# A two-layer graph network on one core: the last row panel's gated unit and its last two tiles by halves, its stores on the load queue, and another order of the row panels

## The chip, the cores and the metric

The kernel runs on one core of a Trainium2 chip. The metric is the device time of one execution, in microseconds (us). Before the change it was 1813.91 us, the median of three runs (1813.1 to 1814.12).

## What is computed

The inputs are `x` (8192 x 128), a weighted adjacency matrix `adj` (8192 x 8192, fp32, 256 MB) and small weights. Cut to what matters:

```python
# layer 0: degree-normalised aggregation, residual, layer norm
dinv = rsqrt(sum(adj, axis=1) + 1e-6)
x1 = layernorm(x + (dinv[:, None] * (adj + I) * dinv[None, :]) @ (x @ W0))
# layer 1: aggregation, message, gated recurrent unit, residual, layer norm
agg = adj @ x1
msg = relu(agg @ W_msg.T + b_msg)
r = sigmoid(msg @ Wir.T + x1 @ Whr.T + b_r)
z = sigmoid(msg @ Wiz.T + x1 @ Whz.T + b_z)
n = tanh(msg @ Win.T + b_in + r * (x1 @ Whn.T + b_hn))
out = layernorm(x1 + (1 - z) * n + z * x1)
```

## The kernel before

**Tiles.** The rows are cut into 16 row panels of W = 512 rows; a tile (i, k) is the 512 x 512 block of row panel i and neighbour panel k, 1 MB, loaded transposed so that the 512 output rows are the free dimension. Features are on the 128 partitions. The matrix is read twice. The first pass (to about 680 us) sums the degrees and already multiplies what it can for layer 0. The second pass is a list `T2` of 256 tiles, one index n per tile: tiles 0 to 103 (N2 = 104) serve layer 0 and layer 1, tiles 104 to 255 (NN = 256) layer 1 alone, row panel after row panel in the order `rows3` (line 183).

**One tile of the second pass.** SP loads it in two halves of 512 KB (L380). ACT writes its rounded part `hi` in fp32r (L678), DVE the rest `lo` = tile - hi (L826), and PE does three products for each of the four 128-row chunks c, hi with x1's high part (L495), lo with the high part (L496), hi with x1's low part (L497): twelve matmuls 512 columns wide, each with its own 128 x 128 weights. `hi` has three buffers: ACT writes tile n when PE is done with tile n - 3. The accumulator `acc1` alternates between two PSUM banks (6 and 1) from row panel to row panel.

**The gated unit of a row panel.** When the last tile of panel i is multiplied (index `gru_at[i]`, lines 192 to 195; at least 9 tiles after that of the panel before), its steps are dealt out over the following tile indices, on each engine behind the tile work of that index: x1 transposed back by eight 128-column products with an identity (`x1t_step`, PE +1, L552 and L554), its copies `x1t` and `x1th` (ACT +5, L714, L715) and `x1tl` (DVE +5, L913), the aggregate `tall` (DVE +3, L902), the message (`msg_step`, PE +4, L562, fp32), the three products with the state (`h_step`, PE +5) and with the message (`gates_step`, PE +6; nine matmuls each, L566 to L568), the two sigmoids (ACT +9, L728, L729), the candidate's two DVE steps (+9, L925, L928), tanh (ACT +11, L733), the new state in three dependent DVE steps (+11, L936, L938, L940), its transpose by four 128 x 128 products (`rows_step`, PE +11, L594), statistics (DVE +14, L835, L839), the reciprocal deviation on POOL (L1041, L1043), the scaling to `y` (DVE +16, L845), and the store, 256 KB, issued by POOL's software queue (L1055). Each of these steps has 512 columns, or four times 128.

After tile 255 nothing is left but the steps of the last panel (panel 7, `gru_at` = 256) and the rest of panel 8's (`gru_at` = 247): the loops run on to index NN + TAIL with TAIL = 17. At the end POOL waits for the stores (L1057), every engine drains, and a barrier (L229) ends the kernel.

**Order.** Each engine works off its own list in order, and the only coupling are semaphores. SP's list holds the loads alone. POOL's holds the deviations and stores. The lines that set the row order and the places of the unit:

```python
    rows3 = [15, 0, 14, 1, 13, 2, 12, 3, 11, 4, 10, 5, 9, 6, 8, 7]
    gru_at, g = {}, -100
    for i in rows3:
        g = max(end3[i], g + 9)
        gru_at[i] = g
    TAIL = gru_at[rows3[-1]] + 17 - NN
```

By these lines the sixteen units stand at 119, 128, 139, 148, 157, 166, 175, 184, 193, 202, 211, 220, 229, 238, 247 and 256.

Of the kernel before, what the change touches and what calls it, by code (L numbers as in the profile page):

```python
# [5 lines left out]
def gnn_resnorm_kernel(nc, adj_blocks, x_t, x, w0, wmsg_t, b_msg, wih_t, whh_t, b_ih, b_hh, out):  # L6
    f32, f32r = mybir.dt.float32, mybir.dt.float32r
    ALU, ACT = mybir.AluOpType, mybir.ActivationFunctionType

    D = 128  # L10
# [182 lines left out]
    for i in rows3:  # L193
        g = max(end3[i], g + 9)
        gru_at[i] = g
    TAIL = gru_at[rows3[-1]] + 17 - NN

    norm_rows = whole[::-1] + rows2
    norm_no = {i: q for q, i in enumerate(norm_rows)}
# [3 lines left out]
        return next((i for i in rows2 if end2[i] + d == n), None)  # L203

    def gru_row(n, d):
        return next((i for i in rows3 if gru_at[i] + d == n), None)

    RING2, RING3 = [0, 1, 2, 3], [0, 1, 2, 3, 15, 16]
    slot_of2, before2, loads2 = [], [], []
# [19 lines left out]
    with ctx:  # L229
# [3 lines left out]
        def sem(name):  # L233
            return ctx.enter_context(nc.semaphore(name))
# [127 lines left out]
        nmul_done, npre_ready, n_ready = sem("nmul_done"), sem("npre_ready"), sem("n_ready")  # L362
        diff_done, new_ready, rows_done = sem("diff_done"), sem("new_ready"), sem("rows_done")
        out_ready = sem("out_ready")

        def group_left(eng, g):

# [5 lines left out]
        @block.sync  # L373
        def _(sp):
            def load(s, i, k):

                P, Q, rows = i // 2, k // 2, (i % 2) * W
                for h in range(2):
                    src = adj_blocks[P * 8 + (P - Q) % 8, 2 * (k % 2) + h, :, :, rows:rows + W]
                    sp.dma_start(raw(s)[:, 2 * h:2 * h + 2, :], src).then_inc(slot_in[s], 16)  # L380

            def load_xt(P):
                if P:
                    sp.wait_ge(supp_done, P)
# [24 lines left out]


        @block.tensor
        def _(pe):
# [175 lines left out]
            def rows_step(i):  # L588
                g = gru_no[i]
                pe.wait_ge(new_ready, g + 1)  # L590
                if g:
                    pe.wait_ge(out_ready, g)
                for c in range(KC):
                    mm = pe.transpose(p_rows[:, c * D:(c + 1) * D], newt[:, c * 128:(c + 1) * 128], ident[:, :])  # L594
                mm.then_inc(rows_done, 1)


            turn(whole[1])
            for R, j in burst[last][2:]:
# [2 lines left out]
            turn(whole[0])  # L602
            layer0(1)
            layer1(0)
            for n in range(1, NN + TAIL):
                if 2 <= n < N2:
                    layer0(n)
                i = normed_row(n, 1)
                if i is not None:
                    turn(i)  # L610
                if n < NN:
                    layer1(n)
                i = gru_row(n, 1)
                if i is not None:
                    x1t_step(i)
                i = gru_row(n, 4)
                if i is not None:
                    msg_step(i)
                i = gru_row(n, 5)
                if i is not None:  # L620
                    h_step(i)
                i = gru_row(n, 6)
                if i is not None:
                    gates_step(i)
                i = gru_row(n, 11)
                if i is not None:
                    rows_step(i)


        @block.scalar  # L630
        def _(act):
# [99 lines left out]
            def n_step(i):  # L731
                act.wait_ge(npre_ready, gru_no[i] + 1)
                act.activation(gn[:, :], gn[:, :], ACT.Tanh, bias=bih_s[:, 2:3]).then_inc(n_ready, 1)  # L733

            for P in range(NP):
# [9 lines left out]
            x1_hi(whole[1])  # L745
            hi_f0(2)
            x1_hi(whole[0])
            for n in range(3, NN + TAIL):
                if n < NN:
                    hi_tile(n)  # L750
                    hi_f0(n)
# [12 lines left out]
                if i is not None:  # L764
                    msg_step(i)
                i = gru_row(n, 9)
                if i is not None:
                    rz_step(i)
                i = gru_row(n, 11)
                if i is not None:  # L770
                    n_step(i)


        @block.vector
        def _(dve):
# [178 lines left out]
            def half_out(h):  # L954
# [6 lines left out]
                rows = part[:, (2 * groups[g][0] + h) * W:(2 * groups[g][0] + h + 1) * W]  # L961
                dve.tensor_copy(rows, group_bank(g, h)[:, :]).then_inc(last_out, 1)

            split_lo(0)
            split_lo(1)
            own_step(whole[1])
# [10 lines left out]
            for n in range(2, NN + TAIL):  # L977
                if n < NN:
                    split_lo(n)
                i = normed_row(n, 2)  # L980
                if i is not None:
                    tall_step(i)
                    if i // 2 >= SELF_PANELS:
                        own_step(i)
                i = normed_row(n, 3)
                if i is not None:
                    row_step(i)
                i = normed_row(n, 4)
                if i is not None:
                    x1_step(i)  # L990
                i = normed_row(n, 5)
                if i is not None:
                    x1_lo(i)
                i = gru_row(n, 3)
                if i is not None:
                    agg_step(i)
                if n == N2 // 4:
                    split_weights()
                i = gru_row(n, 5)
                if i is not None:  # L1000
# [92 lines left out]
```

## Time and profile before

| | |
|---|---|
| runs | 1813.91 us (median of 3; 1813.1 to 1814.12) |
| profiled execution, its own time | 1815.5 us |
| its span in the trace | 1813.6 us |
| mean granted clock of TensorE | 0.972 |
| PE / DVE / ACT / POOL busy | 92% / 80% / 40% / 8% of the span |
| bytes moved by DMA | 551.11 MB, mean 304 GB/s |

The engines are PE (TensorE matmul; PEld its weight loads, which overlap), DVE (VectorE), ACT (ScalarE), POOL (GpSimd) and SP (SyncE, which issues loads). L826 is line 826 of the kernel. The span runs from the first to the last instruction of the trace; the execution's own time is 1.9 us longer, and a difference between two kernels is read in either. A chain of waits is followed back from the last instruction. A timeline lists instructions with start and duration; the duration of a matmul runs to its last result, so back-to-back matmuls overlap, and the distance of two starts is what one costs.

### The profile page before, as it was taken

The numbers are of one execution on the slowest core, as the hardware profiler recorded it, in microseconds if no ns is written. First come the engines' busy times: TensorE is split into PE (matmuls) and PEld (weight loads), VectorE is DVE, ScalarE is ACT, GpSimd is POOL, SyncE is SP. The second block draws the span as 40 slices with busy tenths as digits, with TensorE's granted clock in tenths as the row PEclk, the third lists the DMA queues.
The fourth block names the chain that finished last, engine by engine and source line by source line (L and its number), as shares of the span: only waits on it lengthen the run. The fifth ranks groups of instructions, "written<-read, shape, count | busy, mean of one in ns | idle before, by whom it ended". The sixth has DMA issues, their size and how long they took to land.

```text
span 1813.6 us, 16909 instructions
## 1 busy us (share of the span) xinstructions
PE 1665.1 (92%) x6400; PEld 1167.1 (64%) x6400; DVE 1448.2 (80%) x1372; ACT 725.6 (40%) x708; POOL 141.5 (8%) x110
## 2 busy tenths in 40 slices
PE   0088799997999999999999999999999999999996
PEld 0043254443444456888888888888788888888884
DVE  7888899999999967776666665665789898988886
ACT  0000011111111123544444444444677676767663
POOL 0000000000000011100000000000002112121212
PEclk8589999999999999999999999999999999999998
DMA  9999999999999982666666666665999999999991
GB/s 389 421 380 422 422 421 422 421 421 422 421 421 421 420 311 85 207 200 204 193 196 199 201 190 195 201 192 188 346 344 322 302 320 308 322 312 317 312 313 52
DMA packets 180928, 551.11 MB, mean 304 GB/s; under 512 B 13424, under 2 KB 13936, under 8 KB 148080
## 3 DMA queue, kind: packets, MB, share of 16 engines
q1 hardware_dynamic: 177280, 541.11, 80.8%
q0 software_dynamic: 2560, 8.39, 1.4%
q8 instruction: 51, 0.84, 0.2%
q10 hardware_dynamic: 1008, 0.53, 0.1%
q14 instruction: 29, 0.24, 0.0%
HBM read 545.79 MB, written 4.19 MB: 303 GB/s over the span
## 4 chain that ended last, share of the span: by engine, by line
PE 82%; DMA 13%; DVE 3%; ACT 1%; issue 0%; POOL 0%; SPq 0%; DVEq 0%; ACTq 0%; POOLq 0%
PE bank L444 21%; PE bank L495 18%; PE bank L497 18%; PE bank L496 18%; DMA kept<-adj_blocks 6%; DMA ring<-adj_blocks 4%; DMA pool<-adj_blocks 3%; PE bank L568 1%; PE bank L566 1%; PE bank L567 1%; DVE colsum L804 1%; PE bank L427 1%; PE bank L418 1%; PE bank L562 1%; PE bank L466 1%; DVE lo L826 0%
## 5 line engine op out<-in xcount | busy, mean ns | idle before, releaser
L826 DVE TENSOR_TENSOR lo<-ring,hi 128x2048 fp32r<-128x2048 f32 x206 | 470.3, 2289 | 249.1 <-ACT f L689 205.0
L678 ACT ACTIVATE hi<-ring 128x2048 fp32r<-128x2048 f32 x206 | 395.3, 1919 | 366.8 <-DMA ring<-adj_blocks 238.4
L495 PE MATMUL bank<-hi,x1s 128*128 128x512 f32 x1024 | 409.4, 400 | 3.8 <-DVE lo L826 2.7
L497 PE MATMUL bank<-hi,x1s 128*128 128x512 f32 x1024 | 399.9, 391 | 0.0
L496 PE MATMUL bank<-lo,x1s 128*128 128x512 f32 x824 | 321.6, 390 | 0.0
L444 PE MATMUL bank<-kept,feat 128*128 128x512 f32 x656 | 292.6, 598 | 20.4 <-DMA kept<-adj_blocks 20.4
L444 PEld LDWEIGHTS bank<-kept,feat 128*128 128x128 f32 x656 | 123.4, 191 | 180.6 <-issue 155.0
L804 DVE TENSOR_TENSOR colsum<-colsum,kept 128x2048 f32<-128x2048 f32 x93 | 213.2, 2292 | 20.0 <-DMA kept<-adj_blocks 18.4
L495 PEld LDWEIGHTS bank<-hi,x1s 128*128 128x128 f32 x1024 | 192.7, 188 | 47.1 <-issue 3.6
L497 PEld LDWEIGHTS bank<-hi,x1s 128*128 128x128 f32 x1024 | 192.6, 188 | 41.1
L656 ACT ACTIVATE part<-bank 128x512 f32<-128x512 f32 x72 | 39.1, 595 | 444.5 <-PE bank L444 444.5
L496 PEld LDWEIGHTS bank<-lo,x1s 128*128 128x128 f32 x824 | 155.2, 188 | 33.1 <-issue 1.7
L495 PE MATMUL bank<-hi,f 128*128 128x512 f32 x416 | 162.4, 390 | 0.0
L497 PE MATMUL bank<-hi,f 128*128 128x512 f32 x416 | 161.9, 389 | 0.0
L496 PE MATMUL bank<-lo,f 128*128 128x512 f32 x416 | 161.8, 389 | 0.0
L444 PE MATMUL bank<-ring,feat 128*128 128x512 f32 x272 | 123.8, 601 | 5.8 <-DMA ring<-adj_blocks 5.8
L826 DVE TENSOR_TENSOR more_lo<-more,hi 128x2048 fp32r<-128x2048 f32 x50 | 114.2, 2285 | 14.1 <-ACT hi L678 14.1
L444 PE MATMUL bank<-pool,feat 128*128 128x512 f32 x256 | 115.3, 595 | 6.8 <-DMA pool<-adj_blocks 6.8
L678 ACT ACTIVATE hi<-more 128x2048 fp32r<-128x2048 f32 x50 | 96.0, 1919 | 50.9 <-PE bank L497 48.4
L1041 POOL TENSOR_TENSOR var<-mv,eps_ln 128x4 f32<-128x4 f32 x32 | 36.0, 1126 | 978.9 <-DVE mv L839 978.9
L444 PEld LDWEIGHTS bank<-ring,feat 128*128 128x128 f32 x272 | 51.6, 192 | 71.5 <-issue 61.7
L804 DVE TENSOR_TENSOR colsum<-colsum,ring 128x2048 f32<-128x2048 f32 x38 | 87.1, 2292 | 9.3 <-DMA ring<-adj_blocks 8.7
(111 smaller groups left out, 1689.2 us busy)
## 6 DMA issues: line engine op xcount, KB each, us to landing
ring<-adj_blocks SPq DMA_DIRECT2D x412, 512.0 KB, 5.3
kept<-adj_blocks SPq DMA_DIRECT2D x147, 1024.0 KB, 14.9
ring<-adj_blocks SPq DMA_DIRECT2D x56, 1024.0 KB, 14.9
pool<-adj_blocks SPq DMA_DIRECT2D x53, 1024.0 KB, 14.6
more<-adj_blocks SPq DMA_DIRECT2D x100, 512.0 KB, 5.8
xt<-x_t SPq DMA_DIRECT2D x8, 512.0 KB, 14.1
xin<-x POOLq DMA_DIRECT2D x16, 256.0 KB, 3.4
out<-y POOLq DMA_DIRECT2D x16, 256.0 KB, 3.7
```

The lines of the kernel that those rows point to most:

```text
L418: mm = pe.matmul(p_supp[c // KC][:, (c % KC) * D:(c % KC + 1) * D], xt[:, c * 128:(c + 1) * 128], w0_s[:, :], start=True, stop=True)
L427: mm = pe.matmul(p_deg[:, b:b + 1], csum[:, b * 128:(b + 1) * 128], ones[:, :], start=True, stop=True)
L444: mm = pe.matmul(group_bank(g, h)[:, :], feat0[:, j * 2 + u, :], unit(slot_of1[n])[:, u, h * W:(h + 1) * W], start=begins and g < NP and u ...
L466: mm = pe.matmul(group_bank(g, h)[:, :], feat0[:, j * 2 + u, :], unit(slot_of1[n])[:, u, h * W:(h + 1) * W], start=False, stop=j == 4 * P ...
L495: pe.matmul(acc[:, :], fh, ah, start=start and c == 0, stop=False, skip_group_check=True)
L496: pe.matmul(acc[:, :], fh, al, start=False, stop=False, skip_group_check=True)
L497: mm = pe.matmul(acc[:, :], fl, ah, start=False, stop=stop and c == KC - 1, skip_group_check=True)
L656: ins = act.activation(part[:, i * W:(i + 1) * W], group_bank(g, h)[:, :], ACT.Copy)
L678: ins = act.activation(hi[:, n % NHI], raw(slot_of2[n]), ACT.Copy)
L804: dve.tensor_tensor(cs, cs, slot(slot_of1[n]), ALU.add).then_inc(sum_done, 1)
L826: ins = dve.tensor_tensor(flat(low(n)), flat(raw(slot_of2[n])), flat(hi[:, n % NHI]).bitcast(f32), ALU.subtract)
L1041: pool.tensor_tensor(var[:, at % 2], mv[:, at % 2, :, 1:2], eps_ln[:, :, :], ALU.add).then_inc(veps_ready, 1)
```

## The change

- The row order `rows3` becomes 10, 2, 12, 0, 11, 1, 14, 7, 3, 4, 15, 6, 8, 5, 9, 13. The units now stand at 115, 124, 133, ... 241, nine apart without exception, and the last panel is 13, with 14 tiles (242 to 255).
- The last panel's unit is written out apart. Its `x1t_step` is at PE's index 252. Its last two tiles are multiplied for columns 0 to 255 first, then for columns 256 to 511, the second time into the other accumulator bank; `last_sum` adds both halves' sum so far, `last_sum2` what the second bank holds.
- All its steps but the x1 copies are done for each half of 256 columns, in other banks (`p_rz2`, `p_n2`, `p_msg2`), interleaved in an order given by hand. The new state takes two steps after tanh instead of three, `(gz - 2) * x1t` before it.
- Its two stores of 128 KB are issued by SP, which has no loads left by then; SP waits for them. POOL waits for the other panels' stores.
- TAIL becomes 2.

```diff
-    rows3 = [15, 0, 14, 1, 13, 2, 12, 3, 11, 4, 10, 5, 9, 6, 8, 7]
+    rows3 = [10, 2, 12, 0, 11, 1, 14, 7, 3, 4, 15, 6, 8, 5, 9, 13]
-    TAIL = gru_at[rows3[-1]] + 17 - NN
+    last_row, G, HW = rows3[-1], NT - 1, W // 2
+    TAIL = gru_at[rows3[-2]] + 17 - NN
+        p_rz2, p_n2, p_msg2 = (bank[0], bank[7]), (bank[2], bank[3]), (bank[4], bank[5])
...
@@ sync
+            for h in range(2):
+                c = last_row * KC + 2 * h
+                sp.wait_ge(out_ready, G + 1 + h)
+                sp.dma_start(out_rows[:, c:c + 2, :], y[:, G % 2, 2 * h:2 * h + 2, :]).then_inc(last_stored, 16)
+            sp.wait_ge(last_stored, 32)
@@ tensor
+            def last_tile(n, h):
+                acc, k = acc1[(len(rows2) + G + h) % 2], T2[n][1]
+                pe.wait_ge(lo_ready, n + 1)
+                if h == 1:
+                    pe.wait_ge(agg_ready, G)
+                for c in range(KC):
+                    ah, al = hi[:, n % NHI, c, half(h)], low(n)[:, c, half(h)]
+                    fh, fl = x1s[:, k * KC + c, 0, :], x1s[:, k * KC + c, 1, :]
+                    pe.matmul(acc[:, half(h)], fh, ah, start=h == 1 and n == NN - 2 and c == 0, stop=False,
+                              skip_group_check=True)
+                    pe.matmul(acc[:, half(h)], fh, al, start=False, stop=False, skip_group_check=True)
+                    mm = pe.matmul(acc[:, half(h)], fl, ah, start=False, stop=n == NN - 1 and c == KC - 1,
+                                   skip_group_check=True)
+                if n == NN - 1:
+                    mm.then_inc(halves_done, 1)
...
-            for n in range(1, NN + TAIL):
+            for n in range(1, NN - 2):
...
+                if n == NN - 4:
+                    x1t_step(last_row)
+            last_tile(NN - 2, 0)
+            last_tile(NN - 1, 0)
+            last_h(0)
+            last_msg(0)
+            last_h(1)
+            last_tile(NN - 2, 1)
+            last_gates(0)
+            last_tile(NN - 1, 1)
+            last_msg(1)
+            last_rows(0)
+            last_gates(1)
+            last_rows(1)
@@ scalar
+            x1t_step(last_row)
+            last_relu(0)
+            last_rz(0)
+            last_n(0)
+            last_relu(1)
+            last_rz(1)
+            last_n(1)
@@ vector
+            def last_npre(h):
+                dve.wait_ge(rz_ready, G + 1 + 2 * h)
+                dve.wait_ge(diff_done, 2 * G)
+                dve.scalar_tensor_tensor(gn[:, half(h)], p_n2[h][:, half(1)], bhh_s[:, 2:3], gr[:, half(h)], ALU.add, ALU.mult)\
+                   .then_inc(nmul_done, 1)
+                dve.wait_ge(nmul_done, G + 1 + h)
+                dve.tensor_tensor(gn[:, half(h)], gn[:, half(h)], p_n2[h][:, half(0)], ALU.add).then_inc(npre_ready, 1)
+                dve.wait_ge(rz_ready, G + 2 + 2 * h)
+                dve.wait_ge(rows_done, G)
+                dve.scalar_tensor_tensor(newt[:, half(h)], gz[:, half(h)], -2.0, x1t[:, half(h)], ALU.add, ALU.mult)\
+                   .then_inc(last_u, 1)
...
+                if n == NN - 1:
+                    x1t_lo(last_row)
                 i = gru_row(n, 14)
                 if i is not None:
                     out_stats(i)
+                if n == NN:
+                    last_sum()
                 i = gru_row(n, 16)
                 if i is not None:
                     out_step(i)
+            last_lo(0)
+            last_npre(0)
+            last_sum2()
+            last_newt(0)
+            last_lo(1)
+            last_norm(0)
+            last_npre(1)
+            last_newt(1)
+            last_norm(1)
@@ gpsimd
-            for g, i in enumerate(rows3):
+            for g, i in enumerate(rows3[:-1]):
...
-            for s in range(2):
-                pool.wait_ge(stored[s], NT // 2 * 16)
+            for h in range(2):
...
+            pool.wait_ge(stored[0], NT // 2 * 16)
+            pool.wait_ge(stored[1], (NT // 2 - 1) * 16)
```

`last_h`, `last_msg`, `last_gates`, `last_rows`, `last_relu`, `last_rz`, `last_n`, `last_lo`, `last_newt` and `last_norm` are the steps of the unit named above for one half: nine, one, nine and two matmuls on PE, two, two and one activations, one DVE step for the low part of the message, two for the new state, and two statistics, two aggregates and two scalings.

## Rows read from the trace of the kernel before

**Rows 1.** The page: span, and PE's granted clock in 40 slices.
```profile
span 1813.6 us, 16909 instructions
...
PEclk8589999999999999999999999999999999999998
```

**Rows 2.** Busy time by stretch, 1380 to 1790 us and behind.
```profile
core 0: us, PE busy (x) PEld busy (x) DVE busy (x) ACT busy (x) POOL busy (x), PEclk, DMA share, GB/s
1380.00:1790.00 410.00, 409.94 (x1855) 334.80 (x1854) 365.16 (x382) 277.18 (x209) 74.63 (x39) 1.00 0.90 303
1790.00:1800.68 10.68, 6.17 (x26) 4.00 (x25) 5.71 (x18) 4.34 (x7) 2.01 (x3) 1.00 0.08 25
1800.68:1813.60 12.92, 1.11 (x4) 0.71 (x4) 4.67 (x15) 0.00 (x0) 2.02 (x3) 0.50 0.07 20
```

**Rows 3.** Waits, 1330 to 1789 us: total us, times, longest us.
```profile
ACT hi L678 <- PE bank L497: 137.5, 130, 2.9
DVE lo L826 <- ACT hi L678: 30.8, 29, 2.5
...
PEld bank L495 <- DVE lo L826: 0.3, 1, 0.3
```

**Rows 4.** Chain of waits behind 1790 us: start, us, what.
```profile
1791.45 1.10 PE bank L562 x2
...
1797.07 0.69 ACT gr L728
...
1802.83 1.13 PE bank L594 x4
...
1808.16 0.74 issue
1808.90 0.80 POOL out L1055
```

**Rows 5.** Timeline of PE at the last tile's end: start, us.
```profile
1788.95 0.39 PE L497 MATMUL bank<-hi,x1s 128*128 128x512 f32 x1
1789.18 0.22 PE L552 MATMUL bank<-identr,x1s 128*128 128x128 f32 x1
1789.24 0.27 PE L554 MATMUL bank<-identr,x1s 128*128 128x128 f32 x1
...
1790.02 0.63 PE L594 MATMUL bank<-ident,newt 128*128 128x128 f32 x4
```

**Rows 6.** Instructions of the closing barrier, L229: ns, start us.
```profile
L229 SPq DRAIN  x1: 369/369/369, 1768.7 to 1768.7; - x1
...
L229 POOLq DRAIN  x1: 1462/1462/1462, 1811.9 to 1811.9; - x1
```

**Rows 7.** Instruction groups by shape, whole run: busy us, mean ns.
```profile
L826 DVE TENSOR_TENSOR lo<-ring,hi 128x2048 fp32r<-128x2048 f32 x206 | 470.3, 2289 | 249.1 <-ACT f L689 205.0 <-ACT hi L678 44.1
L678 ACT ACTIVATE hi<-ring 128x2048 fp32r<-128x2048 f32 x206 | 395.3, 1919 | 366.8 <-DMA ring<-adj_blocks 238.4 <-PE bank L497 128.4
...
L723 ACT ACTIVATE msgh<-bank,bmsg_s 128x512 fp32r<-128x512 f32 x16 | 10.9, 680 | 0.0
...
L902 DVE TENSOR_TENSOR tall<-part,bank 128x512 f32<-128x512 f32 x14 | 9.5, 681 | 0.0
```

**Rows 8.** Timeline of DVE, last statistics and scaling.
```profile
1803.98 0.89 DVE L835 BATCH_NORM_STATS2 stats<-bank 128x6 f32<-128x128 f32 x4 [1.21 <-PE bank L594]
...
1806.78 1.37 DVE L845 TENSOR_SCALAR y<-bank,mv,rstd 128x128 f32<-128x128 f32 x4 [1.49 <-POOL rstd L1043]
```

**Rows 9.** Issue to landing, us: POOL's last store, SP's 512 KB loads (L380).
```profile
DMA to landing us min/median/max: 2.8/2.8/2.8
...
L380 SPq DMA_DIRECT2D ring<-adj_blocks x412: 539/604/1587, 646.7 to 1768.0; - x138
...
DMA to landing us min/median/max: 4.0/5.4/15.6
```

**Rows 10.** DMA, GB/s in 40 slices of 0.05 us from 0.75 us.
```profile
GB/s 0 0 0 0 0 0 0 0 0 0 0 0 0 0 0 0 0 0 0 0 655 492 164 0 0 0 0 0 492 655 164 0 0 0 0 0 0 0 0 0
```

More of the change, by code:

```diff
@@ L195, in gnn_resnorm_kernel @@
         gru_at[i] = g
-    TAIL = gru_at[rows3[-1]] + 17 - NN
+    last_row, G, HW = rows3[-1], NT - 1, W // 2
+    TAIL = gru_at[rows3[-2]] + 17 - NN
+    assert end3[last_row] == NN - 1 and last_row in rows2 and gru_at[rows3[-2]] + 11 <= NN - 4
     norm_rows = whole[::-1] + rows2
@@ L205, in gru_row, with half @@
     def gru_row(n, d):
-        return next((i for i in rows3 if gru_at[i] + d == n), None)
+        return next((i for i in rows3[:-1] if gru_at[i] + d == n), None)
+    def half(h):
+        return slice(h * HW, (h + 1) * HW)
     RING2, RING3 = [0, 1, 2, 3], [0, 1, 2, 3, 15, 16]
@@ L364, in gnn_resnorm_kernel @@
         out_ready = sem("out_ready")
+        halves_done, half_sum, last_u, last_new, last_stored = (
+            sem("halves_done"), sem("half_sum"), sem("last_u"), sem("last_new"), sem("last_stored"))
         def group_left(eng, g):
@@ new lines, in half_gate, with last_h @@
+            def half_gate(out, wh, wl, q, xh, xl, start, stop):
+                cols = slice(q * D, (q + 1) * D)
+                pe.matmul(out, wh[:, cols], xh, start=start, stop=False, skip_group_check=True)
+                pe.matmul(out, wh[:, cols], xl, start=False, stop=False, skip_group_check=True)
+                return pe.matmul(out, wl[:, cols], xh, start=False, stop=stop, skip_group_check=True)
+            def last_h(h):
+                xh, xl = x1th[:, half(h)], x1tl[:, half(h)]
+                pe.wait_ge(x1t_split, G + 1)
+                pe.wait_ge(npre_ready, G)
+                half_gate(p_rz2[h][:, half(0)], whhh_s, whhl_s, 0, xh, xl, True, False)
+                half_gate(p_rz2[h][:, half(1)], whhh_s, whhl_s, 1, xh, xl, False, False)
+                half_gate(p_n2[h][:, half(1)], whhh_s, whhl_s, 2, xh, xl, True, False)
@@ new lines, in last_msg, with last_gates @@
+            def last_msg(h):
+                pe.wait_ge(agg_ready, G + 1 + h)
+                if h == 0:
+                    pe.wait_ge(x1t_ready, G + 1)
+                else:
+                    pe.wait_ge(out_ready, G)
+                pe.matmul(p_msg2[h][:, half(0)], wmsg_s[:, :], tall[:, half(h)], start=True, stop=True).then_inc(msg_done, 1)
+            def last_gates(h):
+                mh, ml = msgh[:, half(h)], msgl[:, half(h)]
+                pe.wait_ge(msg_split, G + 1 + h)
+                half_gate(p_rz2[h][:, half(0)], wihh_s, wihl_s, 0, mh, ml, False, True)
+                half_gate(p_rz2[h][:, half(1)], wihh_s, wihl_s, 1, mh, ml, False, True)
+                half_gate(p_n2[h][:, half(0)], wihh_s, wihl_s, 2, mh, ml, False, True).then_inc(gates_done, 1)
@@ L598, in _, with last_rows @@
+            def last_rows(h):
+                pe.wait_ge(last_new, h + 1)
+                for c in range(2):
+                    mm = pe.transpose(p_msg2[h][:, c * D:(c + 1) * D], newt[:, h * HW + c * 128:h * HW + (c + 1) * 128],
+                                      ident[:, :])
+                mm.then_inc(rows_done, 1)
             turn(whole[1])
@@ L610, in _ @@
                     turn(i)
-                if n < NN:
+                if n < NN - 2:
                     layer1(n)
@@ L747, in _ @@
             x1_hi(whole[0])
[L748 to L751, printed above, removed]
+            for n in range(3, NN):
+                hi_tile(n)
+                hi_f0(n)
                 i = normed_row(n, 3)
@@ L962, in half_out, with last_sum @@
                 dve.tensor_copy(rows, group_bank(g, h)[:, :]).then_inc(last_out, 1)
+            def last_sum():
+                i, acc = last_row, acc1[(len(rows2) + G) % 2]
+                dve.wait_ge(halves_done, 1)
+                dve.wait_ge(msg_done, G)
+                dve.wait_ge(spilled, rows2.index(i) + 1)
+                dve.tensor_tensor(tall[:, half(0)], part[:, i * W:i * W + HW], acc[:, half(0)], ALU.add).then_inc(agg_ready, 1)
+                dve.tensor_tensor(tall[:, half(1)], part[:, i * W + HW:(i + 1) * W], acc[:, half(1)], ALU.add)\
+                   .then_inc(half_sum, 1)
@@ new lines, in last_sum2, with last_lo @@
+            def last_sum2():
+                dve.wait_ge(halves_done, 2)
+                dve.wait_ge(half_sum, 1)
+                dve.tensor_tensor(tall[:, half(1)], tall[:, half(1)], acc1[(len(rows2) + G + 1) % 2][:, half(1)], ALU.add)\
+                   .then_inc(agg_ready, 1)
+            def last_lo(h):
+                dve.wait_ge(msg_ready, 2 * G + 2 + 2 * h)
+                dve.tensor_tensor(msgl[:, half(h)], msgt[:, half(h)], msgh[:, half(h)].bitcast(f32), ALU.subtract)\
+                   .then_inc(msg_split, 1)
@@ new lines, in last_newt, with last_norm @@
+            def last_newt(h):
+                dve.wait_ge(n_ready, G + 1 + h)
+                dve.tensor_tensor(gn[:, half(h)], gn[:, half(h)], gz[:, half(h)], ALU.mult).then_inc(diff_done, 1)
+                dve.wait_ge(last_u, h + 1)
+                dve.wait_ge(diff_done, 2 * G + 1 + h)
+                dve.tensor_tensor(newt[:, half(h)], gn[:, half(h)], newt[:, half(h)], ALU.subtract).then_inc(last_new, 1)
+            def last_norm(h):
+                at = NT + G
+                dve.wait_ge(rows_done, G + 1 + h)
+                for c in range(2):
+                    ins = dve.bn_stats(stats[:, at % 2, 2 * h + c, :], p_msg2[h][:, c * D:(c + 1) * D])
+                ins.then_inc(stats_ready, 1)
+                dve.wait_ge(stats_ready, at + 1 + h)
+                for c in range(2):
+                    ins = dve.bn_aggr(mv[:, at % 2, 2 * h + c, :], stats[:, at % 2, 2 * h + c, :])
+                ins.then_inc(var_ready, 1)
+                dve.wait_ge(rstd_ready, at + 1 + h)
+                dve.wait_ge(stored[G % 2], (G // 2) * 16)
+                for c in range(2):
+                    ins = dve.tensor_scalar(y[:, G % 2, 2 * h + c, :], p_msg2[h][:, c * D:(c + 1) * D],
+                                            mv[:, at % 2, 2 * h + c, 0:1], rstd[:, at % 2, 2 * h + c, :],
+                                            ALU.subtract, ALU.mult)
+                ins.then_inc(out_ready, 1)
```

19 lines of the change are left out of this document (added).

## The prediction

> **What bounds the kernel now.** The page comes first: TensorE's granted clock is full nearly everywhere but at the two ends [rows 1]. Then the busy time by stretch: from 1380 to 1790 us PE is busy 409.94 of 410 us, DVE 89%, and the DMA engines 0.90 [rows 2]. The waits of that stage confirm who leads: ACT waits 130 times for a matmul and DVE for ACT, while PE waited once for DVE, 0.3 us [rows 3]. So PE sets the pace until the last tile is multiplied. The tiles end at 1789.18 us, where the timeline turns from L497 to the last panel's x1 products [rows 5]. What follows is one chain through all engines to 1813.6 us, 24.4 us long, in which PE does only 30 matmuls [rows 2, 4]. The change can pay only in that chain and must not disturb the part before.
>
> **Row order.** One tile costs PE 12 x 0.227 = 2.72 us and DVE about 2.2 us (2289 ns busy, starts overlapping a little) [rows 5, 7]. A unit costs PE 6.3 us (x1 0.84, message 0.86, of 1.10 to its result [rows 4], eighteen matmuls 4.15, transposes 0.46) and DVE 8.0 (seven steps of 0.6 to 0.75, a second step of the candidate 0.7, statistics 1.3, scaling 1.3). With a unit each nine tiles that is 30.8 us for PE against 27.8 for DVE. Before, fourteen of the fifteen gaps were nine already (one was 11); now all are. PE still leads with 3 us to spare per unit, and its total work is the same whatever the order: I put the order at 0. If that cover were gone, each microsecond by which a unit were late would cost a microsecond, at each of fifteen units. The order's effect is that panel 9's unit (at 241) is over on PE by index 252, and that panel 13's fourteen tiles lie behind it.
>
> **Where the tail begins.** Let t = 0 be the start of the halved tiles. PE did two tiles (5.45) less than at 1789.18, but the x1 products (1789.18 to 1790.02, 0.84) and panel 9's transposes (0.48, four at 0.11 and a late start behind them) now lie ahead: 1789.18 - 5.45 + 0.84 + 0.48 = **1785.1 us**. ACT writes the last `hi` after tile 252, DVE its `lo` by t = 0.4, needed at 1.4; the copies of x1 are done by 1.0, needed at 2.9. So moving x1 up removes about 2.3 us of chain (1789.18 to 1791.45 [rows 4, 5]) and costs PE nothing new.
>
> **Price of a half.** The trace has no 256-column matmul of this kind. With 512 columns one costs 0.227 us: 0.213 for 512 columns at 2.4 GHz, and 0.014. With 128 columns and new weights each, it costs (1790.02 - 1789.24) / 7 = 0.111, and where the weights were there already, 0.06 (1789.18 to 1789.24) [rows 5]. So 256 columns lie between 0.111 and 0.227; I take **0.12** (0.107 + 0.014), since weights can be had each 0.111. DVE's fixed part is small: (2289 - 681) / 1536 = 1.05 ns per column, so half a step takes 0.41 us instead of 0.68; ACT in the same way 0.47 instead of 0.68 [rows 7]. Two statistics with aggregates take 0.45 + 0.22, two scalings 0.73 (0.32 apart, the last 0.41 [rows 8]). POOL's two steps stay at 1.3 us, hops between engines at 0.03 to 0.1.
>
> **The tail, in t.** PE: tiles 254 and 255, first half, to 2.9; state products to 4.0; message (half of 0.86) to 4.45 with its result at 4.65; state products of half 1 to 5.5; tile 254 second half to 7.0; gates of half 0 to 8.05; tile 255 second half to 9.5. The sum (3.1 to 3.5), panel 9's scaling (to 5.2 on DVE), the two relus (4.7 to 5.5) and the message's low part (to 6.0) lie beside it; the low part is needed at 7.0. Sigmoids of half 0 8.3 to 9.15; the candidate 8.8 to 9.75, DVE's third step to 10.1, and only then `last_sum2` to 10.45: PE has waited 0.9 us. Message of half 1, result 11.15; relus to 12.0, low part to 12.45; PE gates of half 1 12.5 to 13.6; sigmoids from 13.9, the first ready at 14.35. Meanwhile tanh of half 0 ends at 10.3, its new state at 11.2, its transposes at 11.7; DVE then is in `last_norm(0)`: statistics to 13.1, a wait for POOL to 14.5, scaling to 15.3. **The candidate of half 1 is queued behind that wait**, so it starts at 15.3, not 14.4: 0.9 us of the gain is given back. Then candidate to 16.25, tanh to 16.8, new state to 17.7, two transposes to 18.5 (the clock: PE idles from 13.6 to 17.7; before, it was idle from 1797.0, the grant fell to half, 1.2 GHz, at 1800.68 [rows 2], and four transposes took 1.13 us instead of 0.63 [rows 4, 5], so I take the slow price), statistics to 19.2, POOL to 20.6, scaling to **21.4**.
>
> **The store.** Before, the last `y` was ready at 1808.16, POOL's issue began 0.74 later, the landing came 2.8 after that, at 1811.7, and the kernel ended 1.9 us later, 1.46 of them POOL's drain [rows 4, 6, 9]: 5.45 us in all. Now SP issues 0.03 after `y`. The trace has no store by SP: the upper end is its smallest 512 KB load, 4.0 us among other loads [rows 9], less the 1.3 us that 384 KB more take at that stage's 303 GB/s [rows 2], 2.7; the lower end 1.0 us from issue to first data (0.75 to 1.75 us [rows 10]) and 0.4 for 128 KB, 1.4. I take 2.0, nearer to the low end because nothing else moves. The first half's store lies beside the second half. The close: SP's drain was 0.37 [rows 6] and POOL's can run while half 1 is stored, since POOL's last step ends at 20.6 and its waits are long met: 0.6 us (bounds 0.4 and 1.9). Together **2.7 us**, between 1.8 and 4.6.
>
> **Sum.** 1785.1 + 21.4 + 2.7 = 1809.2 against 1813.6: **-4.4 us**, of which about 2.75 are the store and the close, the rest the shorter chain (1808.16 becomes 1806.5). On the profiled execution's own time that is 1815.5 - 4.4 = 1811.1; the median of the runs lies 1.6 below that execution, so the forecast is 1813.91 - 4.4 = **1809.5 us**.
>
> **Rivals.**
> (A) *The issuing queue saves only its issue.* If POOL's drain or its like still ends last, the close stays at 1.9 and the landing at 2.8: 2.0 us less gain, about 1811.5, no measurable change. For it: a drain of 1.46 us on record. Against it: POOL has 3 us before SP's landing. 0.12. The Trainium skill (DMA: Bandwidth & Descriptors, "Issuing engines are not separate DMA queues") says that another issuing engine saves only the sequencer's time for the initiation, little beside the transfer; by that rule this rival holds, and rows 4 speak against it only in that the initiation here was 0.74 plus 0.80 us.
> (B) *Weight loads set the pace*, 0.188 us as the loads' own duration is: 84 half matmuls lie on the chain, 84 x 0.068 less 0.4 of slack = 5.3 more, 1814.8, no change. Against it: 0.111 in rows 5. 0.07.
> (C) *A half costs as much as a whole*, 0.227, whether by the clock or per instruction: 84 x 0.107 less 0.4 = 8.6, and message and transposes 0.4: 9.0 more, **1818.5, slower**. It decides from 0.22 us a matmul on; at 0.16 the gain is 1.4 us. For it: PE pauses at 9.5, 11.7 and 13.6, and the grant did fall in this tail. Against it: the longest pause before 13.6 is 0.9 us, and after 0.8 us of idling before the message at 1791.45 the matmuls to 1797 ran at full grant [rows 2, 4]. 0.05. The Trainium skill (TensorE: Matmul & The Clock Gate, "Why this matters for your kernels") warns of matmuls thinner than 512 rows, whose clock oscillates unless they run back to back; by that rule this rival holds here, and the full grant through the 128-wide products of rows 5 speaks against it.
> (D) *The row order costs PE waits*, from POOL or DVE late at 14 units: 0.6 us at each is 8.4, 1818, slower; a third of it is no change. 0.03.
>
> **Numbers.** Under 0.2% (3.6 us) a measurement of this kernel can't tell a difference, so the line is at 1810.3. The forecast itself, with the matmul between 0.111 and 0.15 and the store between its bounds, spreads from 1807.3 to 1811.5 and holds 0.73; about 0.05 of it lies above the line. With A, B and C's milder part: faster 0.68, no change 0.26, slower 0.06. The range is 1807.4 to 1812.4: it takes in the forecast and A and leaves out B, C and D.
>
> **What would show it.** In the new profile: PE busy to about 1785 without waits; half matmuls 0.12 us apart; PE waiting some 0.9 us for `last_sum2`; DVE waiting over 1 us for POOL's rstd in `last_norm(0)` with the sigmoid of half 1 already done; last `y` near 1806.5; SP's second issue 0.03 later with a landing in about 2; POOL's drain over before it. A later last tile would speak for D, starts 0.19 or 0.23 apart for B or C, a drain of POOL behind the landing for A. The prediction is wrong if the tail from 1785 on is longer than 26 us or shorter than 22.

## The result, and the profile after

The changed kernel takes **1808.93 us** (median of ten runs, 1807.51 to 1810.2), the kernel before 1814.24 us in the ten runs of the same comparisons (1813.1 to 1816.15): ratio 0.9971, 95% interval 0.9963 to 0.998, or 5.3 us less. The forecast was 4.4 us less and 1809.5 us. The profiled execution took 1809.21 us with a span of 1807.4, 6.2 us under the span of before.

Page, busy time by stretch and waits of the changed kernel answer to [rows 1 to 3]:

```profile
span 1807.4 us, 17022 instructions
...
PEclk8589999999999999999999999999999999999998
```
```profile
core 0: us, PE busy (x) PEld busy (x) DVE busy (x) ACT busy (x) POOL busy (x), PEclk, DMA share, GB/s
1380.00:1780.00 400.00, 400.00 (x1803) 326.45 (x1802) 357.65 (x376) 275.09 (x208) 76.53 (x39) 1.00 0.93 311
1780.00:1797.42 17.42, 15.69 (x112) 14.15 (x111) 12.96 (x30) 5.91 (x10) 2.01 (x3) 1.00 0.05 16
1797.42:1807.40 9.98, 2.00 (x9) 1.31 (x7) 4.31 (x15) 1.34 (x3) 1.79 (x4) 0.50 0.09 27
```
```profile
ACT hi L761 <- PE bank L513: 139.6, 132, 2.9
DVE lo L931 <- ACT hi L761: 31.0, 31, 2.5
```

From 1380 to 1780 us the picture is that of before: PE is busy without a gap, ACT waits for it and DVE for ACT, as before. What changed lies behind, in the timeline of the tail. PE first (start, us, instruction; L622 to L625 are tile columns, L632 to L634 state and gates, L650 the message, L662 the transposes):

```profile
1784.50 0.28 PE L622 MATMUL bank<-hi,x1s 128*128 128x256 f32 x1
1784.62 0.28 PE L624 MATMUL bank<-lo,x1s 128*128 128x256 f32 x1
...
1793.74 0.28 PE L625 MATMUL bank<-hi,x1s 128*128 128x256 f32 x1
1794.79 0.70 PE L650 MATMUL bank<-tall,wmsg_s 128*128 128x256 f32 x2 [0.77 <-DVE tall L1082]
1795.66 0.44 PE L662 MATMUL bank<-ident,newt 128*128 128x128 f32 x2 [0.17 <-DVE newt L1108]
1796.88 0.39 PE L632 MATMUL bank<-msgh,wihh_s 128*128 128x256 f32 x1 [0.79 <-DVE msgl L1087]
...
1797.89 0.41 PE L632 MATMUL bank<-msgh,wihh_s 128*128 128x256 f32 x1
1798.11 0.41 PE L633 MATMUL bank<-msgl,wihh_s 128*128 128x256 f32 x1
...
1801.80 0.69 PE L662 MATMUL bank<-ident,newt 128*128 128x128 f32 x2 [3.07 <-DVE newt L1108]
```

Two half matmuls start 0.12 us apart. PE then waits 0.77 us for `last_sum2` and 0.79 for the message's low part, and from 1797.42 its grant (the clock that TensorE is granted) is half: starts 0.21 apart in the later gates of half 1. DVE in the same stretch, and POOL's last deviation:

```profile
1793.99 0.42 DVE L1100 SCALAR_TENSOR_TENSOR newt<-gz,x1t 128x256 f32<-128x256 f32 x1
1794.33 0.41 DVE L1082 TENSOR_TENSOR tall<-tall,bank 128x256 f32<-128x256 f32 x1
...
1798.63 0.73 DVE L1123 TENSOR_SCALAR y<-bank,mv,rstd 128x128 f32<-128x128 f32 x2 [1.11 <-POOL rstd L1238]
1799.28 0.48 DVE L1094 SCALAR_TENSOR_TENSOR gn<-bank,bhh_s,gr 128x256 f32<-128x256 f32 x1
...
1804.39 0.73 DVE L1123 TENSOR_SCALAR y<-bank,mv,rstd 128x128 f32<-128x128 f32 x2 [1.08 <-POOL rstd L1238]
```
```profile
1803.66 0.69 POOL L1238 TENSOR_TENSOR rstd<-var,mhalf 128x2 f32<-128x2 f32 x1
```

The last y is done at 1805.12, 20.6 us behind the first half matmul. The end, which answers to [rows 6, 9], in SP's stores and the closing barrier's instructions (ns, start):

```profile
L423 SPq DMA_DIRECT2D out<-y x2: 389/401/413, 1799.4 to 1805.1; - x2
...
DMA to landing us min/median/max: 1.8/1.9/1.9
```
```profile
L235 POOLq DRAIN  x1: 3147/3147/3147, 1803.8 to 1803.8; - x1
...
L235 SPq DRAIN  x1: 7/7/7, 1807.2 to 1807.2; - x1
```

SP issues at 1805.15, 0.03 behind y, the landing (the store is complete) is at 1807.0, the end at 1807.38: 2.26 us where before it was 5.46. The stretch from the landing to the end is called the close below.

Below, **t** counts from the start of the last two tiles' multiplication (1784.50 here), because executions differ before it: in the eight traces whose code ahead of the tail is the same it begins between 1782.16 (e8) and 1784.50 us. Two more kernels, e3 and e6, have the changed kernel's code up to the last y. In t the last y comes at 20.62 in the changed kernel, 20.62 in e3 and 21.06 in e6, because the grant falls at another place in each (t = 12.9, 14.7 and 12.3). So a difference of under 0.45 us between two single traces shows nothing by itself, unless the steps that make it are followed.

### The profile page after: what moved, and what is told of

It is laid out like the page before. It is cut to its first block, busy times and chain, and to the rows that moved or that the text cites. A ratio compares the mean times of both kernels' runs of the same rounds, so it can differ in the third digit from the quotient of the medians.

```text
span 1807.4 us, 17022 instructions
## 1 busy us (share of the span) xinstructions
PE 1664.8 (92%) x6444; PEld 1169.4 (65%) x6444; DVE 1449.1 (80%) x1380; ACT 726.8 (40%) x713; POOL 138.9 (8%) x111
## 4 chain that ended last, share of the span: by engine, by line
PE 83%; DMA 13%; DVE 3%; POOL 0%; ACT 0%; SPq 0%; issue 0%; DVEq 0%; POOLq 0%; ACTq 0%
PE bank L460 21%; PE bank L511 18%; PE bank L513 18%; PE bank L512 18%; DMA kept<-adj_blocks 6%; DMA ring<-adj_blocks 4%; DMA pool<-adj_blocks 3%; PE bank L584 1%; PE bank L583 1%; PE bank L582 1%; DVE colsum L909 1%; PE bank L443 1%; PE bank L434 1%; PE bank L482 1%; PE bank L578 1%; PE bank L570 0%
## 5 line engine op out<-in xcount | busy, mean ns | idle before, releaser
L460 PE MATMUL bank<-kept,feat 128*128 128x512 f32 x656 | 290.9, 595 | 20.6 <-DMA kept<-adj_blocks 20.6
```

The lines of the kernel that those rows point to most:

```text
L460: mm = pe.matmul(group_bank(g, h)[:, :], feat0[:, j * 2 + u, :], unit(slot_of1[n])[:, u, h * W:(h + 1) * W], start=begins and g < NP and u ...
```

## The experiments

### e1: the store on SP's queue, alone

```diff
 # kernel before
+            sp.wait_ge(out_ready, NT)
+            sp.dma_start(out_rows[:, last_row * KC:(last_row + 1) * KC, :], y[:, 1]).then_inc(last_stored, 16)
+            sp.wait_ge(last_stored, 16)
...
-            for s in range(2):
-                pool.wait_ge(stored[s], NT // 2 * 16)
+            pool.wait_ge(stored[0], NT // 2 * 16)
+            pool.wait_ge(stored[1], (NT // 2 - 1) * 16)
```

> The kernel before, with one thing changed: the last panel's store (256 KB, whole) is issued by SP, and POOL waits only for the other panels' stores. My theory: from the last y to the end 2.8 us instead of 5.45 (0.03 to the issue, about 2.4 to the landing, 0.3 to the close), so 2.6 us less than before. Rival (the issuing queue saves only its issue): 1.5 us less. The last y stays at its place, 18.97 us behind the end of the last tile.

1811.82 us (eleven runs), ratio to before 0.9986 [0.9977, 0.9995], 2.5 to 2.8 us less. The profile puts it where the theory has it: last y at 1807.16, end of span at 1809.91, 2.75 us instead of 5.46. About half of the change's gain is this line. The rival's 1.5 is inside the interval of the runs, but the trace has 2.7.

### e2: x1 early, tiles and unit whole

```diff
 # e1, with the new row order
-    rows3 = [15, 0, 14, 1, 13, 2, 12, 3, 11, 4, 10, 5, 9, 6, 8, 7]
+    rows3 = [10, 2, 12, 0, 11, 1, 14, 7, 3, 4, 15, 6, 8, 5, 9, 13]
...
-                if i is not None:
+                if i is not None and i != rows3[-1]:
                     x1t_step(i)
...
+                if n == NN - 4:
+                    x1t_step(rows3[-1])
...
```

On ACT and DVE the copies and the low part move up in the same way (to index NN - 1).

> The store of e1, the new row order, and the last panel's x1 products, copies and low part early as in the changed kernel, but tiles and unit whole. Theory as the prediction put it (moving x1 up removes 2.3 us of chain): about 4.9 us less than before. Rival, from reading the chain again: the message needs the sum as well, which needs the last tile, and the tile end itself moves 1.3 us later by the x1 products and the transposes ahead of it; the message starts where it started, and the time is that of e1, 2.4 to 2.6 us less than before.

1812.04 us, ratio 0.9986 [0.9977, 0.9995]: the time of e1. The timeline of PE and DVE shows why:

```profile
1790.20 0.39 PE L502 MATMUL bank<-hi,x1s 128*128 128x512 f32 x1
1791.37 1.12 PE L567 MATMUL bank<-tall,wmsg_s 128*128 128x512 f32 x2 [0.78 <-DVE tall L911]
```
```profile
1790.63 0.69 DVE L911 TENSOR_TENSOR tall<-part,bank 128x512 f32<-128x512 f32 x1
```

The message now waits for the 512-wide sum instead of x1's copies and starts 0.94 us behind the tiles' end, where it was 2.27: 1.33 us less. But the tiles end as much later, since x1's products and panel 9's transposes (0.84 + 0.48 us in the prediction's sum) lie ahead of them; in these two executions that is 1790.43 for 1789.18, and the message starts at 1791.37 for 1791.45. So moving x1 up is worth nothing by itself here. In this execution the store landed 3.3 us behind its issue, 2.3 in e1 with the same instruction, and the last y to the end took 3.7 us for e1's 2.75; what held it is open.

### e3: both stores on POOL

```diff
 # changed kernel
-                sp.wait_ge(out_ready, G + 1 + h)
-                sp.dma_start(out_rows[:, c:c + 2, :], y[:, G % 2, 2 * h:2 * h + 2, :]).then_inc(last_stored, 16)
+                pool.wait_ge(out_ready, G + 1 + h)
+                pool.dma_start(out_rows[:, c:c + 2, :], y[:, G % 2, 2 * h:2 * h + 2, :]).then_inc(last_stored, 16)
...
+            pool.wait_ge(last_stored, 32)
```

> The changed kernel, but both stores of the last panel issued by POOL, which waits for them. Theory: 0.75 to the issue, 0.8 issue, landing 0.9 later than SP's, drain of POOL behind the landing: about 3 us more than the changed kernel, 2.3 less than before. Rival (only the issue): 1.5 more than the changed kernel, 3.8 less than before.

1810.41 us, ratio 0.9976 [0.9967, 0.9986], over the changed kernel by 1.5 us in the medians and 0.9 in the ratios to before, whose intervals leave room for the trace's figure. The last y is at the same t; from there to the end it is 4.5 us instead of 2.26, so 2.24 more, between the two expectations. Its parts, from POOL's stores and its drain:

```profile
L1237 POOL DMA_DIRECT2D out<-y x2: 747/760/772, 1799.2 to 1804.6; - x2
...
DMA to landing us min/median/max: 2.2/2.3/2.3
```
```profile
L235 POOLq DRAIN  x1: 1543/1543/1543, 1807.0 to 1807.0; - x1
```

The issue starts 0.30 behind y (0.27 more than SP's), the landing takes 0.4 longer, and the close 1.94 instead of 0.40. The start and the landing are 0.7 us of the 2.24, most of it the issue itself, which takes 0.76 on POOL and 0.40 on SP; the close, with the drain in it, is 1.5. The rule of the Trainium skill behind rival A (DMA: Bandwidth & Descriptors, "Issuing engines are not separate DMA queues"), that another issuing engine saves only the time of the initiation, fits the first part and doesn't cover the second.

This trace has a second use. Its lists are those of the changed kernel up to the last y, but the grant stayed full through half 1's gates; ACT's sigmoid, DVE's candidate and the granted clock (the column before the DMA share) show it:

```profile
1783.65:1798.35 14.70, 11.98 (x91) 10.88 (x89) 9.13 (x30) 3.86 (x9) 2.91 (x5) 1.00 0.06 18
1798.35:1808.80 10.45, 0.69 (x2) 0.29 (x2) 3.61 (x12) 0.51 (x1) 2.42 (x4) 0.50 0.08 26
```
```profile
1797.40 0.47 ACT L821 ACTIVATE gr<-bank,brz 128x256 f32<-128x256 f32 x1 [1.88 <-PE bank L629]
```
```profile
1798.41 0.47 DVE L1089 SCALAR_TENSOR_TENSOR gn<-bank,bhh_s,gr 128x256 f32<-128x256 f32 x1
```

The sigmoid is ready at t = 14.22, 0.52 earlier than in the changed kernel, and DVE comes to the candidate at 14.76, as there (14.78), because it is still in half 0's scaling. The last y gains nothing.

### e6: POOL waits for SP's stores

```diff
 # changed kernel
             pool.wait_ge(stored[1], (NT // 2 - 1) * 16)
+            pool.wait_ge(last_stored, 32)
```

> The changed kernel, POOL waits for SP's two stores as well before it goes to the closing barrier. Theory (POOL's drain behind the landing was a large part of the old close): the landing stays at 1.9 us behind SP's issue, POOL's drain of about 1.5 us then lies behind it, and from the last y to the end it takes 3.8 us instead of 2.26. Rival (the drain is free, the issue was all that counted): 2.3 us as in the changed kernel.

1810.9 us, ratio 0.9978 [0.9969, 0.9988], by the runs 1.3 to 2.0 us over the changed kernel. SP's landing is unchanged (1.8 us), and from the last y to the end it takes 4.95 us, 2.7 more than in the changed kernel and 1.1 more than expected. The drain took longer here than in e3:

```profile
L235 POOLq DRAIN  x1: 2605/2605/2605, 1807.3 to 1807.3; - x1
```

So the drain behind the landing costs 1.5 us (before, e3) to 2.6 (e6), and the larger part of what moving the store brought is that POOL has no wait ahead of it. Why it is longer where POOL's last work was a deviation rather than an issue, no run settles.

### e5: the row order alone

```diff
 # kernel before
-    rows3 = [15, 0, 14, 1, 13, 2, 12, 3, 11, 4, 10, 5, 9, 6, 8, 7]
+    rows3 = [10, 2, 12, 0, 11, 1, 14, 7, 3, 4, 15, 6, 8, 5, 9, 13]
```

> The kernel before with the new row order alone (last panel 13, its unit at 255 instead of 256). Theory: no change. PE never waits in the stage, its work is the same, and the tail is the same chain of 512-wide steps: last y within 0.2 us of 18.97 behind the last tile's end. Rival D (the order costs waits at the units, or frees some): PE would wait for DVE or ACT between 1330 and 1789 us, and the time would move by more than 2 us either way.

1814.58 us against 1814.82, ratio 0.9996 [0.9987, 1.0005]. The last tile ends at 1788.83 and the last y at 1807.80, 18.97 us later as before. In its waits from 1330 to 1789 us PE has none for DVE but one:

```profile
PEld bank L495 <- DVE more_lo L826: 0.3, 1, 0.3
```

### e7: half 0's scaling behind half 1's candidate

```diff
 # changed kernel, DVE's list; last_norm split in statistics and scaling
             last_lo(1)
-            last_norm(0)
+            last_stats(0)
             last_npre(1)
+            last_scale(0)
             last_newt(1)
...
```

> The changed kernel, but DVE scales half 0 to y only behind half 1's candidate, so that it doesn't wait for POOL with half 1's sigmoid done. The prediction put the price of that wait at 0.9 us: by it the last y comes at t = 19.7 instead of 20.6. Rival, from the changed kernel's trace (the sigmoid of half 1 was ready 0.04 us before DVE came to it, since the gates ran at half clock and POOL was quicker than expected): no gain, t = 20.5 to 20.6, the wait only moves.

1808.57 us, ratio 0.9964 [0.9951, 0.9978]. The last y is at t = 20.38, 0.24 earlier, between the two. But in this execution the grant fell only at 1799.52, behind the gates, with the same pauses of PE as in the changed kernel:

```profile
1784.00:1799.52 15.52, 12.01 (x91) 10.88 (x89) 9.81 (x32) 4.13 (x10) 2.91 (x5) 1.00 0.06 17
1799.52:1806.70 7.18, 0.69 (x2) 0.29 (x2) 2.91 (x11) 0.24 (x1) 0.89 (x2) 0.50 0.13 38
```

So the trace to hold beside it is e3's, with the grant full through the gates and the old order. The sigmoid is ready at t = 14.22 in both; DVE takes the candidate at 14.25 instead of 14.76, and 0.3 of these 0.5 us is lost again because the scaling now stands between the candidate and the new state. At full grant, DVE's wait for POOL with the scaling behind it thus cost 0.5 us, not the 0.9 of the prediction, and this reordering gets 0.24 of it.

### e8: matmuls in PE's pauses

```diff
 # changed kernel, PE's list
             last_tile(NN - 1, 1)
+            filler(6)
             last_msg(1)
             last_rows(0)
+            filler(7)
             last_gates(1)
```

`filler(m)` multiplies m times `whhh_s` with 256 columns of x1 into the bank of the old accumulator, which `last_sum` has read.

> The changed kernel with 13 extra matmuls (256 columns, into a bank nobody reads any more) in PE's two pauses ahead of half 1's gates, six before its message and seven behind half 0's transposes. Theory (the pauses bring the granted clock down at 1797.4, in the midst of the gates): the grant stays full through the gates, they stay 0.12 us apart, and the last y is 0.4 to 0.7 us earlier, t = 19.9 to 20.2. Rival (the grant falls at that place whatever PE does there, or the fillers delay what is behind them): t = 20.6 or later.

1808.67 us, ratio 0.9963 [0.9949, 0.9976]. The gates of half 1 stay 0.12 us apart and the grant falls at 1799.2, but the last y is at t = 20.60, 0.02 earlier, and where e3 had it with a full grant and no fillers. DVE's timeline:

```profile
1796.28 0.73 DVE L1131 TENSOR_SCALAR y<-bank,mv,rstd 128x128 f32<-128x128 f32 x2 [1.11 <-POOL rstd L1246]
1796.92 0.47 DVE L1102 SCALAR_TENSOR_TENSOR gn<-bank,bhh_s,gr 128x256 f32<-128x256 f32 x1
```

The sigmoid was ready at 1796.37; DVE was busy with half 0's scaling, for which it had waited 1.11 us, until 1796.92. The rival has the number, by another reason than it gave. That the fillers are what held the grant is not shown either: in e3 and e7 it held through the gates without them. In e6, with the same list for PE as the changed kernel, it fell sooner, at 1796.43; all nine gates of half 1 ran at half the clock, DVE stood waiting for the sigmoid, and the last y came at t = 21.06:

```profile
1799.39 0.48 DVE L1094 SCALAR_TENSOR_TENSOR gn<-bank,bhh_s,gr 128x256 f32<-128x256 f32 x1 [0.36 <-ACT gr L826]
```

### e10: both together

```diff
 # e8, DVE's list
             last_lo(1)
-            last_norm(0)
+            last_stats(0)
             last_npre(1)
             last_newt(1)
+            last_scale(0)
...
```

> The changed kernel with the fillers of e8 and with half 0's scaling behind half 1's new state. Theory (the half clock of the gates and DVE's wait for POOL hide each other: each alone costs nothing, both gone give what half 1's chain takes without them): last y at t = 20.0 to 20.1 instead of 20.6, where e8 alone gave 0 and e7 0.24. Rival (something else holds half 1's candidate): t = 20.4 or more.

1807.6 us, ratio 0.9963 [0.995, 0.9977], last y at t = 19.87: 0.75 us earlier, a little more than expected.

```profile
1797.74 0.48 DVE L1102 SCALAR_TENSOR_TENSOR gn<-bank,bhh_s,gr 128x256 f32<-128x256 f32 x1 [1.25 <-ACT gr L834]
```
```profile
1800.27 0.44 PE L668 MATMUL bank<-ident,newt 128*128 128x128 f32 x2 [3.07 <-DVE newt L1116]
```

Of this, 0.52 us is the candidate (t = 14.26 for 14.78), as in e7 but without the scaling in the way. The other 0.23 is the clock: the grant fell only at 1800.92, behind the last two transposes, which took 0.44 us instead of 0.69. So two costs of half a microsecond, the gates at half clock and DVE's wait for POOL with the scaling behind it, lie beside each other in the changed kernel: without the first alone the last y stays (e3, e8), without both the candidate comes 0.5 us earlier (e7, e10). That the second alone would give nothing is read from the changed kernel's times (the sigmoid was ready 0.04 us before DVE came); no run has the new order with the gates at half clock. The runs' times don't tell e7, e8 and e10 apart, nor clearly from the changed kernel (their ratios are 0.9963 or 0.9964, its 0.9971): these readings rest on one trace each.

### e4: the tiles first

```diff
 # changed kernel, PE's list; last_tile takes all 512 columns
             last_tile(NN - 2, 0)
             last_tile(NN - 1, 0)
             last_h(0)
             last_msg(0)
+            last_msg(1)
             last_h(1)
-            last_tile(NN - 2, 1)
             last_gates(0)
-            last_tile(NN - 1, 1)
-            last_msg(1)
-            last_rows(0)
             last_gates(1)
+            last_rows(0)
             last_rows(1)
```

ACT and DVE take each step for half 0 and half 1 in turn; `last_sum2` is gone.

> The changed kernel, but the last two tiles are multiplied whole (24 matmuls of 512 columns) before anything of the unit, the unit stays in halves: state 0, message 0, message 1, state 1, gates 0, gates 1, rows 0, rows 1; DVE and ACT take each step for both halves one after the other. Theory: what ends last in the changed kernel is the chain of half 1, which starts only when its tile columns are done at t = 9.5; with whole tiles both halves start at 5.5, the gates of half 1 end near 10.8 instead of 14.0, the last y is at about 18.0 instead of 20.6, and the time is 2.6 us less than the changed kernel, 7.9 less than before. Rival (the overlap of half 1's tiles with half 0's unit is what pays): no better than the changed kernel, at best 5.3 less than before, or worse by up to 2.5.

**1805.81 us** (five runs, 1805.26 to 1807.7), ratio to before 0.9955 [0.9942, 0.9967], 3.1 us under the changed kernel by the medians, 8.8 under before by them and 8.2 by the ratio. The last y is at t = 18.02, where 18.0 was expected. PE and DVE:

```profile
1789.46 0.39 PE L622 MATMUL bank<-hi,x1s 128*128 128x512 f32 x1
...
1792.55 0.28 PE L631 MATMUL bank<-x1th,whhl_s 128*128 128x256 f32 x1
1792.73 0.39 PE L629 MATMUL bank<-msgh,wihh_s 128*128 128x256 f32 x1
...
1794.84 0.28 PE L631 MATMUL bank<-msgh,wihl_s 128*128 128x256 f32 x1
```
```profile
1794.61 0.48 DVE L1089 SCALAR_TENSOR_TENSOR gn<-bank,bhh_s,gr 128x256 f32<-128x256 f32 x1 [1.20 <-ACT gr L821]
...
1798.37 0.43 DVE L1103 TENSOR_TENSOR newt<-gn,newt 128x256 f32<-128x256 f32 x1
```

PE works without a gap of over 0.1 us, and the last gate matmul starts at t = 10.6, where it was 13.8 in the changed kernel: the state products of both halves fill the way from the sum through relu to the low part, and half 1's own way starts at 5.4 instead of 9.4. Behind that DVE works through ten steps in a row, to the last new state.

Not all of the 2.6 us in t is the order of the tiles. Half 0's scaling stands behind half 1's new state here too, and the transposes run at full grant (0.44 us), which together were worth 0.75 us in e10. Against e10 the last y is 1.85 us earlier (18.02 for 19.87); that is left for the whole tiles and the new turns on ACT and DVE, which no run separates.

### e9: a step of DVE's to POOL

```diff
 # e4; on POOL ahead of the two deviations, for both halves
-                dve.scalar_tensor_tensor(newt[:, half(h)], gz[:, half(h)], -2.0, x1t[:, half(h)], ALU.add, ALU.mult)
+                pool.tensor_scalar(newt[:, half(h)], gz[:, half(h)], -2.0, None, ALU.add).then_inc(last_u, 1)
+                pool.wait_ge(last_u, 2 * h + 1)
+                pool.tensor_tensor(newt[:, half(h)], newt[:, half(h)], x1t[:, half(h)], ALU.mult).then_inc(last_u, 1)
...
```

> The kernel of e4, with (gz - 2) * x1t of both halves on POOL, in two steps each, instead of one step each on DVE. Theory (in e4 DVE works without a pause from its first candidate step at 1794.61 to half 1's new state at 1798.80, so two steps of 0.34 us less there move the end by as much): last y 0.6 us earlier than in e4, 17.4 behind the start of the last two tiles instead of 18.0. Rival (POOL's two steps take over 1 us each half and the new state waits for them): no gain or up to 1 us later.

1805.69 us, ratio 0.9951 [0.9938, 0.9965], not to be told from e4; the last y is at t = 18.16, 0.14 later. The rival: POOL's two steps take 1.7 us for what DVE does in 0.42, and half 1's new state waits 0.68 for them.

```profile
1796.15 1.02 POOL L1230 TENSOR_SCALAR newt<-gz 128x256 f32<-128x256 f32 x1
1797.26 0.72 POOL L1232 TENSOR_TENSOR newt<-newt,x1t 128x256 f32<-128x256 f32 x1
```

## Why the prediction was right, and where not

**What bounds it and the row order**: right. PE leads to the last tile in both, and the order alone is worth nothing that the runs can tell (e5); rival D is out. One count was misread: 30 matmuls are those from 1790 us on, and from the tiles' end at 1789.18 there are 36; no sum uses it.

**Where the tail begins**: forecast 1785.1, found 1784.5. All eight traces with this code ahead of the tail begin it before 1785.1 (1782.16 to 1784.50); the forecast was laid on one execution of the kernel before, which had itself taken 1.6 us more than the median.

**"Moving x1 up removes about 2.3 us of chain"**: wrong as a part. e2 shows 0. The message needs the later of x1's copies and the sum. Before, the sum was ready at 1790.28 and the copies at 1791.31; with x1 early the copies are there, but the tiles end later by what was moved ahead of them, and the sum is ready at 1791.32. The forecast's total didn't contain the 2.3, since the tail was laid out anew step by step; whoever adds up such parts would have promised e2 2.3 us that aren't there.

**A half matmul at 0.12 us**: right, 0.12 from 1784.50 to 1797.42; B is out, and so is C as put, a whole's price for all 84. But its clock did come in for the last five gates of half 1, 0.21 apart, where the forecast had the grant fall only behind 13.6. **Half steps at 0.41 and 0.47 us**: right (0.41 to 0.42 and 0.47). **PE's 0.9 us wait for the sum**: 0.77. POOL's deviation was taken at 1.3 us and takes 0.96 for half the columns: once ahead of half 1's candidate and once at the end, that is 0.7 of the 0.8 us by which the last y was early, t = 20.6 for 21.4.

**"0.9 us of the gain is given back" by DVE's wait for POOL**: the wait is there (1.11 us), its price is not. The sign that was named, the sigmoid of half 1 already done while DVE waits for POOL, isn't in this trace: DVE came to half 1's candidate at 1799.28, 0.04 behind the sigmoid, because the gates had partly run at the half clock and POOL was quicker. In e3's, with the grant full, the sigmoid is ready 0.1 us behind the end of the wait (1797.87 for 1797.77) and DVE comes 0.5 us later still, from the scaling. The forecast charged 0.9 for wait and scaling and missed the half clock of the gates, which lie beside each other; that the candidate came near its time (t = 14.78 for 15.3) is in that part luck.

**The store and the close**: 2.7 forecast, 2.26 measured; e1 has 2.75 for 256 KB. Landing 1.8 to 1.9 for 2.0, close 0.40 for 0.6. The reason was only half right: POOL's drain was to be over before the landing, but took 3.15 us and ended with it, at about 1807.0. Rival A (the queue saves only its issue) is out by e1, e3 and e6: two thirds of e3's 2.24 us are the close.

**The sum**: forecast -4.4, measured -5.3 by the medians. Between the two profiled executions it is -6.2: 3.2 from the store and the close, where 2.75 was forecast, and 3.0 from the last y, where 1.65 was forecast. Of the 1.35 more on the last y, 0.55 is the earlier start of the tail in this execution and 0.8 the shorter tail. From the start of the tail to the end it took 22.9 us, inside the 22 to 26 that the prediction gave itself.

**What the forecast didn't ask** is whether this interleaving is a good one. Its own layout had the answer: half 1's tile columns end at 9.5, and everything that ends last comes behind them. e4 takes that away and, with a better place for the scaling, gains as much again as all of the change but the store (3.1 us by the medians, against 5.3 less e1's 2.75).

## What to carry to other kernels

Cutting a tail into halves pays by the half that ends last: put the work that both need (here the tiles) first, and fill the latencies of the chain with independent work (the state products), rather than finishing half 0 while half 1's inputs are still to be made. Price a moved step by what else its consumer waits for. Two costs beside each other hide each other: an experiment that removes one and shows nothing has not shown it free. And look at more than one trace of the same code before a few tenths of a microsecond are put down to an edit.

## What was not expected of the hardware

The closing drain of POOL took 1.46 and 1.54 us behind a landing it had issued itself (the kernel before, e3), 2.60 behind one of SP's (e6), and 3.15 to 3.48 where it began while the last deviation still ran (the changed kernel and e4; e1, with four columns). Counted from that deviation's end, these three drains ran on for about 2.6 us, as in e6, where the last work on POOL was a deviation too; why, no run settles. In the changed kernel and in e4 the drain ends within 0.1 us of SP's landing, so by these traces (an estimate) a faster store would bring 0.1 us at most there. And the grant to PE fell at t = 12.3 (e6), 12.9 (the changed kernel), 14.7 (e3) and 15.5 (e7) with the same instructions on PE and the same pauses up to half 1's gates; the last y moved by 0.44 us between e6 and the changed kernel, whose lists up to it are the same.
